# Latent values of two heads at once, made directly as [keys, values]

## The reference, cut to what matters

```python
x = layernorm(hidden)                         # [1, 1024, 512], fp32
q  = (x @ w_q)                                # 32 heads of 128
k, v = x @ w_k, x @ w_v                       # 8 key/value heads, each for 4 query heads
lk = (x @ w_lq) @ w_lk                        # latent keys,   32 heads of 128
lv = x @ w_lv                                 # latent values, 32 heads of 128
q, k, lk = rope(q), rope(k), rope(lk)
attn = causal_attention(q, k, v)              # ordinary
lat  = causal_attention(q, lk, lv)            # latent, same queries
hidden = hidden + attn @ w_o + lat @ w_lo
hidden = hidden + ffn(layernorm(hidden))      # W, b, and a routed low-rank part
```

## Time and profile before

| | us |
|---|---|
| three runs | 2184.62, 2184.03, 2177.3 (median 2184.03) |
| span of the profiled execution, first to last instruction | 2180.9 |
| a head without new keys and values | 60.8 |
| a head with them (hh 3, with the loop's turn) | 76.5 to 77.4 |

### The profile page before, as it was taken

One profiled execution on the slowest core, in us unless ns is written; L12 is line 12 of the kernel. 1 busy time (PEld: TensorE's weight loads), 2 busy tenths in 40 slices (PEclk: granted clock), 3 DMA queues, 4 the chain that ended last, 5 costly groups with the idle time before them and its releaser, 6 DMA issues.

```text
span 2180.9 us, 37717 instructions
## 1 busy us (share of the span) xinstructions
PE 2099.1 (96%) x11236; PEld 1757.8 (81%) x11236; DVE 1582.3 (73%) x2946; ACT 1141.3 (52%) x2502; POOL 884.5 (41%) x693
## 2 busy tenths in 40 slices
PE   5999999999999999999999999999999999999989
PEld 4888878888788887888888887888878888888877
DVE  6677767777777777777767776777777777777775
ACT  2555545555455555556455554555545555455541
POOL 4333443434533344443533444333453434444311
PEclk9999999999999999999999999999999999999999
DMA  2111111111111111111111111111111111111121
GB/s 94 36 35 36 38 30 41 41 36 45 27 41 27 41 46 31 41 31 41 36 35 34 39 36 32 41 39 38 44 28 41 27 41 46 30 41 31 41 50 39
DMA packets 101898, 84.34 MB, mean 39 GB/s; under 512 B 28200, under 2 KB 73896, under 8 KB 101680
## 3 DMA queue, kind: packets, MB, share of 16 engines
q1 hardware_dynamic: 101680, 81.65, 15.3%
HBM read 79.26 MB, written 2.36 MB: 37 GB/s over the span
## 4 chain that ended last, share of the span: by engine, by line
PE 69%; DVE 14%; issue 10%; POOL 3%; ACT 3%; DVEq 0%; DMA 0%; ACTq 0%; SPq 0%; POOLq 0%
PE scores L415 9%; PE scores L417 8%; PE scores L416 8%; PE bankT L477 8%; PE bankX L415 7%; PE bankX L417 6%; PE bankX L416 6%; PE bankO L415 5%; PE bankO L417 5%; PE bankO L416 5%; DVE rot_half L980 3%; DVE rot_half L979 3%; DVE probs L963 3%; DVE PT_lo L969 2%; DVE o_raw L1034 1%
## 5 line engine op out<-in xcount | busy, mean ns | idle before, releaser
L703 ACT ACTIVATE PT_hi<-bankT 128x512 fp32r<-128x512 f32 (+2 forms) x640 | 337.0, 533 | 424.2 <-PE bankO L417 356.4
L969 DVE TENSOR_TENSOR PT_lo<-bankT,PT_hi 128x512 fp32r<-128x512 f32 (+2 forms) x640 | 387.7, 609 | 196.6 <-ACT PT_hi L703 191.6
L762 ACT ACTIVATE probs<-probs,nmax 128x128 f32<-128x128 f32 (+7 forms) x512 | 394.8, 773 | 140.5 <-DVE nmax L963 140.1
L963 DVE CUSTOM_DVE_ANT_0 probs<-scores,mask 128x128 f32<-128x128 f32 (+7 forms) x512 | 381.0, 750 | 64.6 <-PE scores L417 61.8
L477 PE MATMUL bankT<-ident,probs 128*128 128x128 f32 x2304 | 381.9, 275 | 10.3 <-ACT probs L762 4.4
L477 PEld LDWEIGHTS bankT<-ident,probs 128*128 128x128 f32 x2304 | 280.9, 140 | 93.6 <-ACT probs L762 18.6
L1197 POOL TENSOR_TENSOR rot<-rot,cos 128x512 f32<-128x512 f32 x144 | 185.7, 1289 | 230.5 <-DVE rot_half L980 230.5
L1191 POOL TENSOR_TENSOR OT_lo<-o_raw,OT_hi 128x512 fp32r<-128x512 f32 x64 | 82.7, 1292 | 411.6 <-ACT OT_hi L703 411.6
L1199 POOL TENSOR_TENSOR rot<-rot,rot_half 128x512 f32<-128x512 f32 x144 | 207.3, 1440 | 11.3
L703 ACT ACTIVATE OT_hi<-o_raw 128x512 fp32r<-128x512 f32 x128 | 80.9, 632 | 187.1 <-DVE o_raw L1034 182.8
L979 DVE TENSOR_TENSOR rot_half<-rot,sin 64x512 f32<-64x512 f32 x144 | 108.8, 755 | 82.8 <-ACT rot L703 79.3
(11 more groups left out here) (241 smaller groups left out, 5213.3 us busy)
## 6 DMA issues: line engine op xcount, KB each, us to landing
inv_b<-inverses SPq DMA_DIRECT2D x128, 256.0 KB, 4.0
stage<-in_L_attn_w_q SPq DMA_DIRECT2D x32, 256.0 KB, 4.4
stage<-in_L_attn_w_lv SPq DMA_DIRECT2D x32, 256.0 KB, 2.7
stage<-in_L_attn_w_o SPq DMA_DIRECT2D x32, 256.0 KB, 4.3
stage<-in_L_attn_w_lo SPq DMA_DIRECT2D x32, 256.0 KB, 2.6
acc<-in_L_attn_hidden_states SPq DMA_DIRECT2D x2, 1024.0 KB, 6.6
stage<-in_L_attn_w_k SPq DMA_DIRECT2D x8, 256.0 KB, 4.5
stage<-in_L_attn_w_v SPq DMA_DIRECT2D x8, 256.0 KB, 4.6
```

Of the source, the lines that this page charges most:

```text
L703: return act.activation(place, src, ACT.Copy)
L762: act.activation(prob_tile(c, t), prob_tile(c, t), ACT.Exp, bias=nmax[:, c, t:t + 1], scale=-1.0, accum_out=rsum[:, c, t:t + 1]).then_inc( ...
L963: dve.tensor_tensor_reduce(place, src, tile_view(mask[:, S - width:S], c), -SCALE, -MASKED, ALU.add, ALU.min, nmax[:, c, t:t + 1]).then_in ...
L969: dve.tensor_tensor(pt_place(1, hh, w, j), bankT[j % 2][:, block_columns(c, j):CH], f32(pt_place(0, hh, w, j)), ALU.subtract).then_inc(pt_ ...
```

## The change

The latent values of heads hh and hh+1 (hh even) are made in one go, with 128x128 tiles of x stationary and 256 columns of `Wlv` (two heads) moving, so that they come out as [keys, values] and need no `vT` copy and no transposes. It takes four pieces LV 0 to 3 of 24 matmuls 128x256 each, all in the even head: LV 0 in w0 slot 3, LV 1, 2 and 3 in w1 slots 0, 3 and 5. The odd head has none. `LV` and `Wlv` are twice as wide; the two halves of `Wlv` are loaded as two loads, Wlv0 and Wlv1, both in w3 of the odd head. Where w1's pieces lie in the banks is written out in `BANKS_W1`. The diff below, cut to its core, is in the order of the file: tables, SP (start, then each head), PE, ACT (each head, then the start), DVE, POOL (w3, then the start, where these calls stand behind the four ropes of the first head).

```diff
     if w == 0:
-        return {0: ("LK", 0), 1: ("LK", 1), 3: ("LV", 0)}
+        latent = {3: ("LV", 0)} if hh % 2 == 0 else {}
+        return {0: ("LK", 0), 1: ("LK", 1), **latent}
     if w == 1:
-        return {0: ("LV", 1), 1: ("OUT1", 0), 2: ("OUT1", 1), 3: ("LVT", 0), 5: ("LVT", 1), 6: ("OUT1", 2),
-                7: ("OUT1", 3)}
+        if hh % 2 == 0:
+            return {0: ("LV", 1), 1: ("OUT1", 0), 2: ("OUT1", 1), 3: ("LV", 2), 5: ("LV", 3), 6: ("OUT1", 2),
+                    7: ("OUT1", 3)}
+        return {0: ("OUT1", 0), 2: ("OUT1", 1), 4: ("OUT1", 2), 6: ("OUT1", 3)}
...
+BANKS_W1 = [{0: 1, 1: 0, 2: 1, 3: 0, 5: 0, 6: 1, 7: 0}, {0: 1, 2: 0, 4: 1, 6: 0}]
...
+def loads_of(hh):
+    keys = ["Wk", "Wv"] if hh == GROUP - 1 else []
+    return keys + ["Wq", "Wo", "Wlo", "Wlk"] + (["Wlv0", "Wlv1"] if hh % 2 else [])
...
-            for no, src in enumerate((columns(w_lq, 0), columns(w_v, 0), w_lk[:, 0:HD], columns(w_lv, 0))):
+            for no, src in enumerate((columns(w_lq, 0), columns(w_v, 0), w_lk[:, 0:HD], columns(w_lv, 0),
+                                      columns(w_lv, HD))):
                 load(no + 2, no % 2, src)
...
                     fetch("Wlk", w_lk[:, bass.ds(after, HD)])
-                    fetch("Wlv", columns(w_lv, after))
+                    if hh % 2:
+                        for k in range(2):
+                            fetch(f"Wlv{k}", columns(w_lv, after + k * HD))
                     spread_inverses(g, hh, 3)
...
+            def latent_values(n, bank):
+                for i in range(2):
+                    place = banksX[bank][:, i * LV_PAIR:(i + 1) * LV_PAIR]
+                    rows = slice((2 * n + i) * P, (2 * n + i + 1) * P)
+                    for k in range(ND):
+                        mm = mm3(place, both(xnT, ALL, k, rows), both(Wlv, ALL, k, ALL), k == 0, k == ND - 1)
+                return mm
...
                 elif name == "LV":
                     pe.wait_ge(w_lo, n_latent_load(g, hh, "Wlv"))
-                    mm = project(Wlv, n, bank)
-                elif name in ("LVT", "VT"):
+                    mm = latent_values(n, bank)
+                elif name == "VT":
                     mm = value_transposes(n, bank)
...
 -                        if w == 3 and s in (5, 6) and more:
-                            name, places = (("Wlk", Wlk), ("Wlv", Wlv))[s - 5]
-                            fetched(g, hh, name, places)
+                        if w == 3 and s == 5 and more:
+                            fetched(g, hh, "Wlk", Wlk)
+                        if w == 3 and s in (6, 7) and more and hh % 2:
+                            fetched(g, hh, f"Wlv{s - 6}", Wlv_half[s - 6])
...
              for n in range(2):
-                value_high(9 + n, V[0], n, n)
+                value_high(9 + n, V[0], n, TPC, n)
+            weights_hi(6, 0, 4, Wlv_half[1])
             block_hi(0, 0, 0, 0)
...
-                elif name in ("VT", "LVT"):
-                    value_lo(vt_no(g, hh, name, n) + 3, V if name == "VT" else LV, n, bank)
+                elif name == "VT":
+                    value_lo(vt_no(g, hh, name, n) + 1, V, n, TPC, bank)
+                elif name == "LV":
+                    value_lo(vt_no(g, hh, name, n) + 1, LV, n, 2, bank)
...
-                        for name, places in (("Wlk", Wlk), ("Wlv", Wlv)):
+                        latent = (("Wlv0", Wlv_half[0]), ("Wlv1", Wlv_half[1])) if hh % 2 else ()
+                        for name, places in (("Wlk", Wlk), *latent):
                             weights_low(load_no(g, hh, name), load_no(0, hh, name) % 2, places)
...
             weights_low(4, 0, Wlk)
-            weights_low(5, 1, Wlv)
+            weights_low(5, 1, Wlv_half[0])
+            weights_low(6, 0, Wlv_half[1])
```

More of the change, by code:

```diff
@@ L57, in pieces_of, with last_out1, last_out1_of_bank @@
     return {**ahead, **{s: ("OUT0", n) for n, s in enumerate(slots)}}
+BANKS_W1 = [{0: 1, 1: 0, 2: 1, 3: 0, 5: 0, 6: 1, 7: 0}, {0: 1, 2: 0, 4: 1, 6: 0}]
+def last_out1(hh):
+    return max(BANKS_W1[hh % 2])
+def last_out1_of_bank(hh, bank):
+    return max(s for s, b in BANKS_W1[hh % 2].items() if b == bank)
 ROPE = ("Q", "K", "LK")
@@ L82 @@
 ROPES_PER_GROUP = 2 * (2 * GROUP + 1)
-VTS_PER_GROUP = 2 * (GROUP + 1)
-LOADS_BEFORE = 6
-LOADS_PER_GROUP = 5 * GROUP + 2
+LV_PAIR = 2 * HD
+LV_PIECES = 4
+VTS_PER_GROUP = LV_PIECES * GROUP // 2 + 2
+VTS_BEFORE = 4
+LOADS_BEFORE = 7
+def loads_of(hh):
+    keys = ["Wk", "Wv"] if hh == GROUP - 1 else []
+    return keys + ["Wq", "Wo", "Wlo", "Wlk"] + (["Wlv0", "Wlv1"] if hh % 2 else [])
+LOADS_PER_GROUP = sum(len(loads_of(hh)) for hh in range(GROUP))
 C_T, C_PV, C_OS, C_OL = 1, 3, 2, 1
@@ L139, in attn_ffn_kernel @@
         Wv = pair("Wv", [P, ND, HD])
-        Wlv = pair("Wlv", [P, ND, HD])
+        Wlv = pair("Wlv", [P, ND, LV_PAIR])
         Wlk = pair("Wlk", [P, HD])
@@ L181, in attn_ffn_kernel @@
         f32 = lambda ap: ap.bitcast(F32)
+        Wlv_half = [[h[:, :, k * HD:(k + 1) * HD] for h in Wlv] for k in range(2)]
+        Wlq = Wlv_half[0]
         def block_no(g, hh, w, j):
@@ L208, in piece_bank @@
         def piece_bank(hh, w, s, more):
-            return sorted(pieces_of(w, hh, more)).index(s) % 2 if w in (1, 3) else 0
+            if w == 1:
+                return BANKS_W1[hh % 2][s]
+            return sorted(pieces_of(w, hh, more)).index(s) % 2 if w == 3 else 0
         def bank_x_taken(eng, g, hh, w, s, last):
@@ L236, in vt_no @@
         def vt_no(g, hh, name, n):
-            return g * VTS_PER_GROUP + (2 + 2 * hh + {"LVT": 0, "VT": 2}[name] + n)
+            return g * VTS_PER_GROUP + (VTS_BEFORE + (2 * hh if name == "LV" else VTS_PER_GROUP - 2) + n)
         def load_no(g, hh, name):
-            order = (["Wk", "Wv"] if hh == GROUP - 1 else []) + ["Wq", "Wo", "Wlo", "Wlk", "Wlv"]
-            return g * LOADS_PER_GROUP + (LOADS_BEFORE + 5 * hh + order.index(name))
+            before = sum(len(loads_of(k)) for k in range(hh))
+            return g * LOADS_PER_GROUP + (LOADS_BEFORE + before + (loads_of(hh).index(name) if name else 0))
         def n_latent_load(g, hh, name):
-            before = g * LOADS_PER_GROUP + (LOADS_BEFORE + 5 * hh)
-            return before - (1 if name == "Wlk" else 0)
+            return load_no(g, hh, "") - (2 if name == "Wlk" and hh % 2 == 0 else 0)
         def tiles_made(g, hh, w):
@@ L486, in pv_block @@
                     pe.wait_ge(o_scaled, unit_no(g, hh, w) + C_OS)
-                values = both(LV if kind else V, ALL, j, ALL)
+                values = both(LV, ALL, j, slice(hh % 2 * HD, (hh % 2 + 1) * HD)) if kind else both(V, ALL, j, ALL)
                 if j == BLOCKS[w] - 1:
@@ L585, in group_of_heads @@
                             transpose_block(g, hh, w, s + 2)
[L586 to L591, removed]
+                        if s == 0 and w == 0 and hh == 0:
+                            pe.wait_ge(x_free, g * FREES_PER_GROUP + FREES_BEFORE)
+                        if hh % 2 == 0 and (w, s) in ((2, 0), (3, TPC)):
+                            pe.wait_ge(x_free, n_free(g, hh, 1, 0 if w == 2 else 5))
                         if s == BLOCKS[w] - 1:
@@ L602, in _ @@
                 normalised_transpose(0, i)
-            places = (Wq, Wk, Wlv, Wv)
+            places = (Wq, Wk, Wlq, Wv)
             for n in range(2):
@@ L752, in rope_high, with value_high @@
                 copy(place, rot[:, slot, :]).then_inc(rope_hi, 1)
-            def value_high(n_x, place, n, bank=0):
+            def value_high(n_x, place, n, tiles, bank=0):
                 act.wait_ge(x_ready, n_x)
-                copy(place[:, n * TPC:(n + 1) * TPC, :], banksX[bank].rearrange("p (k n) -> p k n", k=TPC))\
+                copy(place[:, n * tiles:(n + 1) * tiles, :], banksX[bank].rearrange("p (k n) -> p k n", k=tiles))\
                     .then_inc(v_hi, 1)
@@ L800, in group_of_heads @@
                                       piece_bank(hh, w, s, more))
[L801 to L805, removed]
+                        if name == "LV":
+                            if n == 0:
+                                act.wait_ge(pv_done, block_no(g, hh, 0, 0) + C_PV)
+                            value_high(n_piece(g, hh, w, s), LV[0], n, 2, piece_bank(hh, w, s, more))
                         if w == 3 and s in (2, 3) and more and hh == GROUP - 1:
@@ L854, in _ @@
             normalised_hi(0, range(TPC))
-            weights_hi(2, 0, 2, Wlv)
+            weights_hi(2, 0, 2, Wlq)
             root(1, 1)
@@ L884, in _ @@
             first_high(3)
[L885 removed]
+            weights_hi(5, 1, 3, Wlv_half[0])
             for n in range(2):
[L887 removed]
+                value_high(9 + n, V[0], n, TPC, n)
+            weights_hi(6, 0, 4, Wlv_half[1])
             block_hi(0, 0, 0, 0)
@@ L985, in value_copy, with value_lo @@
                 dve.tensor_copy(vT[:, n * CH:(n + 1) * CH], banksX[bank]).then_inc(x_free, 1)
-            def value_lo(n_v, places, n, bank=0):
```

(7 more changed lines are left out.)

16 lines of the change are left out of this document (7 added, 9 removed).

## The result

The changed kernel takes 2281.64 us (four runs, 2278.68 to 2288.23) against 2184.02 before: a ratio of 1.046, 95% interval 1.0443 to 1.0478, so 97.6 us slower. The direction was forecast, with the likeliest case at 2250; the measured time lies above the range (2205 to 2270), and of the 98 us the sum gave 66.

The account below looks back on a forecast made before the run. PE, busy 96% of a 2180.9 us span, was taken as the bound: 2180.9 - 27.5 - 18.9 + 0 + 44 + 20 + 3 + 42 + 3.8 = 2247.3; the runs' median lies 3.1 higher: 2250 us, range 2205 to 2270.

Parts of the forecast that it names:

- (1): On PE, the four transposes that turn the latent values back go, in 64 pieces: 27.5 us off.
- (2): On PE, LV 1's wait for the bank of LV 0 goes, 0.59 us 32 times: 18.9 us off.
- (3): LV pieces: 24 matmuls of 128x256 cost the same as 12 of 128x512: 0, bounds -4 to +7 us.
- (4): In w0 of odd heads PE stands still until the exponentials; 16 x 2.77 = 44 us of removed work lost.
- (5): In w1 of odd heads PE waits for scale_out and LK 0's low half: 20 us, bounds 10 and 26.
- (6): SyncE's queue in odd heads' w3: inverses stuck behind Wlv1 make scale_out late: 42 us, bounds 26 and 58.
- (7): Once at the start, ACT waits for the sixth load ahead of the first PT_hi: 3.8 us.
- B: Rival: w3's inverses are hidden anyway, the sum without 42: 2208 us; chance 0.10.
- C: Rival: odd heads lose nothing, as DVE and ACT keep up: 2144 us if inverses are hidden too; chance 0.05.
- D: Rival: odd heads lose nothing but the inverses are late: 2186 us, no change; chance 0.05.
- F: Rival: weight loads exposed in long runs of 256s, 0.14 us each, 38 us more: 2288 us; chance 0.02.
- E: Rival: further waits, in even heads or from a code fetch: above 2270 us; chance 0.07.

Follow-up runs that it names:

- e3_odd_filled: Changed kernel with 12 unused 128x512 matmuls put into w0 slot 3 of every odd head: 2276.21 us, ratio 1.0437 to the kernel before.
- e5_out_in_w0: Changed kernel with two of the four output tiles of odd heads moved from w1 into w0 slots 2 and 3: 2232.18 us, ratio 1.0239.
- e8_before_odd_without: Kernel before with the odd heads' latent values left out and OUT1 in w1 slots 0, 2, 4, 6: 2146.16 us, ratio 0.9843.
- e6_wlv1_late: Changed kernel with w3's inverses queued ahead of Wlv1, and Wlv1's halves made in the next even head, also at the start: 2213.05 us, ratio 1.0159.
- e2_before_late_inverses: Kernel before with a Wq load that waits for Wlk_lo queued ahead of w3's inverses in odd heads: 2242.15 us, ratio 1.028.
- e1_inverses_first: Changed kernel with w3's inverses put into SP's queue between Wlv0 and Wlv1, ahead of the wait for Wlk_lo: 2228.88 us, ratio 1.0218.
- e4_before_256: Kernel before with each of LV's 768 matmuls of 128x512 cut into two of 128x256: 2185.12 us, ratio 1.002.

## Why the prediction was off, by its own steps

**(1), (2), (3), right.** No turning back is left, `vT` is waited for at V alone, LV 1 starts without a wait. In the changed kernel a 256 of a long run starts 0.12 us before the next; alone, the cut costs 4.1 us, within -4 to +7.

**(4) and (5), right.** A head of hh 1 takes 58.2 us, against 60.8 before and "near 58" forecast. The waits of 2.93 us (0.16 of it there before), 0.4 and 0.95 are where they were put. But the one for `LKT_lo` was to come 16 times and is printed in 3 heads (see below). e3_odd_filled (44 us of work for nothing), e5_out_in_w0 (48 us won by filling) and e8_before_odd_without (35 us left of 112) agree.

**(6), right in its mechanism, short in its price.** This is the term of the sum that failed: "8 heads of hh 1: 29 us", "1.9 x 7 = 13 us", "Together 42 us". The lateness of `scale_out` was right to 0.1 us at hh 1. The price was taken as the lateness alone, at a clock that stays at 2.4 GHz. It does not stay: PE, which had been kept busy, does almost nothing for 3 us and gets 1.2 GHz for the next 3.4 us. In the changed kernel the one head of hh 2 at full clock takes 68.7 us, 3.7 more than in e6_wlv1_late; the seven with a slow stretch take 70.1 to 71.6. Over the eight that makes 43 us in place of 29, of which 14 are the clock. The turn of the loop gives 19 in place of 13; e2_before_late_inverses shows that its lateness itself was put too low (2.2 to 3.0 at full clock, not 1.9). Together 63 in place of 42, and alone, in e2_before_late_inverses, 60 in the trace.

The Trainium skill ("TensorE: Matmul & The Clock Gate", "Part 1: The HAM clock gate") has this as a rule: the half rate is the default, and only activity lifts it. I priced weight loads by that page and left this rule out, since the trace of before shows a full clock nearly throughout; the trace now agrees with it, 1.00 to 0.50 after the wait. The rival that was missing is not one more wait but the same waits at a second price.

**In the odd heads that second price is next to nothing.** Two heads of hh 1 in the changed kernel, again with the granted clock third from the end:

```profile
130.76:188.99 58.23, 55.08 (x296) 46.42 (x295) 41.69 (x81) 31.96 (x71) 24.00 (x19) 0.97 0.17 38
401.46:459.63 58.17, 54.07 (x297) 45.17 (x296) 41.73 (x81) 31.77 (x71) 23.98 (x19) 1.00 0.17 38
```

Six of the eight have a slow stretch behind the wait for the exponentials and take 58.2 to 58.4 us; the two without take 58.2. The slow matmuls only use up the wait that would have followed: the 3 odd heads where a wait for `LKT_lo` is printed are the 3 at full clock there. So the 9 us of clock that I had put into the expectations of e6_wlv1_late and e8_before_odd_without were not there, and that both came within 2 us of the number with them was luck. By an estimate, matmuls lose 1.4 us in a slow stretch like the one shown (3 x 0.19 + 6 x 0.14), 38 us in the 27 or so that the 92 us more at 1.2 GHz make; the heads show that only some 15 to 20 of that reached the span.

**(7), near.** The first head takes 69.8 us, 4.8 more than in e6_wlv1_late, which has the step removed; 3.8 was summed. PE waits 2.99 us for `PT_lo` there, and a slow stretch follows. PT_hi was to run "near 66" and ran at 63.56, but the whole start came 2.2 us earlier in this execution (first score tile at 53.61, before 55.84), so it was 3.7 us late.

**What is left.** Of the 29.5 us of span that the sum lacked (95.9 - 66.4), (6) has some 21 and (7) one. The rest shows in e6_wlv1_late, which has neither: its heads are longer than the steps give, by 0.2 us each in hh 0, 1 and 2, and by 0.6 in hh 3 (74.4, steps 73.8), some 9 us in all. At hh 3 most of it is a wait that the sum had at 0.2: at the end of w1 the exponentials come 0.7 us late (printed 0.52), in 7 heads. For the 0.2 us of the others no cause is shown; in the even heads it is of the size of what 256 columns cost in e4_before_256.

**Rivals.** B (inverses hidden) fell with e1_inverses_first and e2_before_late_inverses; C (odd heads lose nothing), and D with it, with the trace; F (weight loads) with e4_before_256. What was called E, "further waits", held the right time, above 2270, with a wrong reason and 0.07.

## What to carry to other kernels

Before removing work from the engine that is the bound, look at which wait that work covers: a wait that is exactly covered has no row, and shows only when the end of the supplier is laid beside the start of what needs it. Work that is gathered into every second unit leaves holes in the others; fill these with work whose inputs are ready (here worth 48 us), or the gain stays out. In an in-order DMA queue, put what the end of a stage needs ahead of a load that has to wait for another engine. Price a TensorE wait of some 3 us by its length and by the slower matmuls behind it, but only where dense work follows: here 3.6 us of lateness made a head 4.5 to 6.3 us longer, while behind the odd heads' waits, where PE soon waits for another engine anyway, a slow stretch cost 0.1 us. Compare the lengths of the same unit of work with and without a slow stretch in one trace; the mean clock does not tell which of the two it is.

## What the runs showed of the hardware that was not expected

Waits of PE of 0.5 and 2.8 us, with only two transposes between them, are followed by 3.4 us at a granted clock of 0.50, although PE has been at 1.00 for long before. In those 3.4 us starts of 512-column matmuls lie 0.42 us apart and of 384-column ones 0.32. Waits of the same length in odd heads are followed by it in some heads and not in others: the head of hh 1 shown above, with 2.77, kept its clock.

A 2 KB store issued 0.5 us behind a 256 KB load on the same queue lets its dependent DMA go after 2.43 us, where 1.4 is the median. All 22 such stores of the changed kernel, and the 7 before, take 2.4 to 3.5 us: here small transfers are held up by large ones just ahead of them. Some others, with no load just ahead, take as long (2.39 for the one at 1007.57).
